# Masked keys by halves of an image, and the ends of the segments inside the edge stage of a window-attention, graph and experts kernel

## The reference, cut to what matters

```
x = x + attention(ln_c(x))      # twice over 8x8 windows: unshifted, then shifted by 4 and masked; 8 heads of 16
t = x as (32768, 128)
t = t + ffn(ln_t(t))

ffn(x): h = x @ W_gat                            # (32768, 4 heads, 4 experts)
        src, dst = edges (524288) and a loop at each node
        e = leaky_relu(a_src[src] + a_dst[dst]);  ee = exp(e - segment_max(e, dst))
        agg = segment_sum(h[src] * ee, dst) / segment_sum(ee, dst) + b_gat
        scores = layernorm(agg) averaged over heads; top 2 of 4 experts, softmax w
        out = sum over experts of w_e * (gelu(x @ W1_e + b1_e) @ W2_e + b2_e)
```

## Time and profile before

| | |
|---|---|
| median of 3 runs | 8224.57 us (8219.5 to 8226.58) |
| the profiled execution | 8225.16 us, its span 8223.3 us |
| busy, share of the span | DVE 62%, POOL 59%, PE 52%, PEld 29%, ACT 26% |
| attention, 0 to 2212 us | DVE busy 1965.09 us, PE 1807.92 us |
| edges, 2212 to 7712 us | POOL busy 4162.86 us in 4355 instructions, DVE 2771.32 us |
| 7712 to 7763 us | DVE busy 23.01 us, POOL 3.44 us |
| combine, 7763 us on | DVE busy 328.98 us, DMA engines 69% |

### The profile page before, as it was taken

One profiled execution on the slowest core, in us unless ns is written; L12 is line 12 of the kernel. 1 busy time (PEld: TensorE's weight loads), 2 busy tenths in 40 slices (PEclk: granted clock), 3 DMA queues, 4 the chain that ended last, 5 costly groups with the idle time before them and its releaser, 6 DMA issues. The chain is left out here.

```text
span 8223.3 us, 105909 instructions
## 1 busy us (share of the span) xinstructions
PE 4280.7 (52%) x31501; PEld 2348.5 (29%) x31501; DVE 5088.4 (62%) x15628; ACT 2131.3 (26%) x3826; POOL 4854.7 (59%) x5216
## 2 busy tenths in 40 slices
PE   5888888888643544535445354453544535445200
PEld 3556656556411221212212122121221212212000
DVE  9998889888745545445455454554545445455378
ACT  4666767666300100101001001010100101101034
POOL 2221112111377777777777777777777777777572
PEclk8889999999765665655656556565565655656555
DMA  1111111111211111111111111111111111111267
GB/s 48 51 51 49 50 54 52 49 55 48 62 32 37 38 32 43 32 32 43 32 43 32 32 43 32 43 32 32 43 32 43 32 32 43 32 43 32 80 202 251
DMA packets 537640, 419.78 MB, mean 51 GB/s; under 512 B 177554, under 2 KB 450498, under 8 KB 536642
## 3 DMA queue, kind: packets, MB, share of 16 engines
q1 hardware_dynamic: 323058, 323.88, 11.8%
q0 software_dynamic: 147552, 56.96, 7.0%
q10 hardware_dynamic: 66560, 33.56, 1.4%
HBM read 203.65 MB, written 176.72 MB: 46 GB/s over the span
## 5 line engine op out<-in xcount | busy, mean ns | idle before, releaser
L1326 POOL DMA_INDIRECT edge_G<-node_rows,edge_src x4352 | 4161.1, 956 | 1326.3 <-issue 1326.3
L1363 PE MATMUL edge_cbank<-edge_ohh,edge_ohl 128*128 128x256 bf16 x4096 | 1418.2, 395 | 2951.9 <-DVE edge_ohh L1496 2876.5
L1363 PEld LDWEIGHTS edge_cbank<-edge_ohh,edge_ohl 128*128 128x128 bf16 x4096 | 426.3, 104 | 3937.2 <-DVE edge_ohh L1496 3762.3
L1496 DVE TENSOR_SCALAR edge_ohh<-edge_iob,edge_dlf 128x256 bf16<-128x256 bf16 x4096 | 1196.7, 298 | 0.0
L564 POOL TENSOR_SCALAR attn_nw<-attn_mv 128x8 f32<-128x8 f32 x64 | 86.4, 1350 | 1725.5 <-DVE attn_mv L993 1725.4
L1495 DVE TENSOR_SCALAR edge_ohl<-edge_iob,edge_dlf 128x128 bf16<-128x128 bf16 x4096 | 1087.0, 266 | 14.8 <-DVE edge_dlf L1489 14.5
L1343 ACT ACTIVATE edge_hid<-edge_hbank,edge_b1c 128x512 f32<-128x512 f32 x512 | 351.6, 687 | 2498.2 <-PE edge_hbank L1370 2498.2
L1454 DVE COPY edge_O<-edge_O 128x24 f32<-128x24 f32 x64 | 12.7, 198 | 1534.6 <-DMA edge_G<-node_rows,edge_src 1534.6
L1506 DVE TENSOR_TENSOR edge_yo<-edge_ybank,edge_b2r 128x512 f32<-128x512 f32 x256 | 176.9, 691 | 946.4 <-PE edge_ybank L1379 946.4
L1346 ACT ACTIVATE edge_w<-edge_w 128x272 f32<-128x272 f32 x64 | 27.5, 429 | 2407.0 <-DVE edge_w L1468 2407.0
L1370 PE MATMUL edge_hbank<-edge_xt,edge_w 128*128 128x512 f32 x1024 | 590.2, 726 | 0.4 <-ACT edge_hid L1343 0.4
(11 more groups left out here) (239 smaller groups left out, 6383.1 us busy)
## 6 DMA issues: line engine op xcount, KB each, us to landing
edge_G<-node_rows,edge_src POOLq DMA_INDIRECT x4352, 2.4
expert_out<-edge_yo SPq DMA_DIRECT2D x64, 1024.0 KB
comb_ye<-expert_out SPq DMA_DIRECT2D x32, 2048.0 KB, 12.0
state_rows<-edge_O SPq DMA_DIRECT2D x64, 816.0 KB, 4.2
attn_km<-attn_kT SPq DMA_DIRECT2D x2048, 16.0 KB, 1.8
attn_xin<-in_x SPq DMA_DIRECT2D x32, 512.0 KB, 4.2
attn_xres<-in_x SPq DMA_DIRECT2D x32, 512.0 KB, 5.3
x_rows<-attn_x SPq DMA_DIRECT2D x32, 512.0 KB, 3.1
```

The source lines that it names most:

```text
L1326: pool.indirect_dma_start(G[b][:, t, :], None, node_rows, bass.IndirectOffsetOnAxis(ap=src[b][:, t:t + 1], axis=0)).then_inc(s_g[b][2 * t ...
L1363: pe.matmul(cbank[b][:, 0:HI], ohl[:, t % RING, :], ohh[:, t % RING, :], start=(t == 0), stop=(t == HC - 1)).then_inc(s_ohp, 1)
L1496: dve.tensor_scalar(ohh[:, t % RING, :], iob[:, :], dlf[:, 1, t:t + 1], None, ALU.is_equal).then_inc(s_oh, 1)
```

## The change

The tile of masked keys gets room for both halves of an image (8 windows each) in place of two quarters: 8 heads x 2 halves x 2 streams = 32 transfers of 32 KB in a step. Half 1 of both streams is the first thing that SP issues in a step; half 0 of the next step stands where quarter 0 stood. The block of the ends is gone: POOL makes its constants at the start of the edge block, DVE does the index of the last rows (`end_rows()`) before the scans of the last chunk and the carries (`carried()`) after them, with PE, ACT and POOL appended at the ends of their lists. The last state, first start and counts stay on chip, and so does the index, which combine reads directly. At the start of the edge block SP issues keys before weights, and DVE waits for POOL's 9 constants rather than for the weights. In diff form, cut:

```diff
@@ attention
-KRING = 2
-QWIN = 4
-QUARTERS = WGRID * WGRID // QWIN
+HWIN = WGRID * WGRID // 2
-        km = [sb(f"km{s}", [P, KRING, HEADS // 2, QWIN, WTOK]) for s in range(2)]
+        km = [sb(f"km{s}", [P, 2, HEADS // 2, HWIN, WTOK]) for s in range(2)]
-            def own_rows(s, m, q):
-                st, h, r = STREAM[s], q // 2, q % KRING
-                if q % 2 == 0:
-                    wait_free(sp, f"{s}k{h}", m)
-                if q >= KRING or m > 0:
-                    sp.wait_ge(s_sc, (m + LAG[s]) * PAIRS + 2 * (q - KRING) + 2)
-                c = (q % 2) * QWIN * WTOK
+            def own_rows(s, m, h):
+                st = STREAM[s]
+                wait_free(sp, f"{s}k{h}", m)
+                if m > 0:
+                    sp.wait_ge(s_sc, (m - 1 + LAG[s]) * PAIRS + 4 * h + 4)
                 for head in range(HEADS):
                     lo = head * HDIM
-                    sp.dma_start(km[st][lo:lo + HDIM, r, head % (HEADS // 2), :, :].rearrange("p w k -> p (w k)"),
-                                 kT[st][h][lo:lo + HDIM, c:c + QWIN * WTOK]).then_inc(s_km[st][r], 16)
+                    sp.dma_start(km[st][lo:lo + HDIM, h, head % (HEADS // 2), :, :].rearrange("p w k -> p (w k)"),
+                                 kT[st][h][lo:lo + HDIM, :]).then_inc(s_km[st][h], 16)
...
-                for s in streams(n):
-                    own_rows(s, n - LAG[s], 2)
-                for s in streams(n):
-                    own_rows(s, n - LAG[s], 3)
...
-                        for r in range(KRING):
-                            act.wait_ge(s_km[st][r], KM_DONE * (2 * m - 1 + h))
+                        act.wait_ge(s_km[st][h], KM_DONE * m)
...
-                if j % 2 == 0:
-                    pe.wait_ge(s_km[st][q % KRING], KM_DONE * (2 * m + q // 2 + 1))
+                    pe.wait_ge(s_km[st][h], KM_DONE * (m + 1))
@@ edges, SP
+            load_keys(0, 0)
+            load_keys(1, 1)
+            load_raw(0, 0)
+            load_x(0, 0)
             sp.dma_start(w1[:, :, :], W1.rearrange("e p f -> p e f")).then_inc(s_w, 16)
...
-            load_keys(0, 0)
...
+            sp.wait_ge(s_c, CONSTANTS)
+            sp.dma_start(state_rows[SORTED:SORTED + P, :], zero[:, 0:NROW]).then_inc(s_z, 16)
             chunks(sp, body)
-            sp.dma_start(last_state, O[1][:, TC, :]).then_inc(s_end, 16)
-            sp.dma_start(first_start, fmin[:, :]).then_inc(s_end, 16)
-            sp.wait_ge(s_hs, CHUNKS)
-            sp.dma_start(hist_out, hist[:, :]).then_inc(s_end, 16)
-            sp.wait_ge(s_end, 48)
+            sp.wait_ge(s_z, 16)
+            sp.wait_ge(s_new, 16)
             for b in range(2):
                 sp.wait_ge(s_st[b], 16 * CHUNKS // 2)
                 sp.wait_ge(s_yst[b], 16 * CHUNKS // 2)
@@ edges, DVE
-            dve.wait_ge(s_c, 2)
-            dve.wait_ge(s_w, 64)
+            dve.wait_ge(s_c, CONSTANTS)
...
                 outputs(b, i)
+                if last_of(b, i):
+                    end_rows()
                 st.k = 0
                 math(b, i, at + C)
+                if last_of(b, i):
+                    carried(O[b])
@@ edges, POOL
+            pool.memset(ones[:, :], 1.0).then_inc(s_c, 1)
...
             chunks(pool, body)
+            pool.wait_ge(s_end, mark["row"])
+            for b in range(2):
+                pool.wait_ge(s_st[b], 16 * CHUNKS // 2)
             pool.wait_ge(s_z, 16)
             pool.indirect_dma_start(old[:, :], None, state_rows, bass.IndirectOffsetOnAxis(ap=ri[:, 0:1], axis=0)).then_inc(s_old, 16)
-            pool.wait_ge(s_step, mark["new"])
+            pool.wait_ge(s_end, mark["new"])
             pool.indirect_dma_start(state_rows, bass.IndirectOffsetOnAxis(ap=ri[:, 0:1], axis=0), new[:, :], None).then_inc(s_new, 16)
@@ combine
-            sp.dma_start(ix[:, :], end_rows).then_inc(s_ix, 16)
-            pool.wait_ge(s_ix, 16)
```

More of the change, by code:

```diff
@@ L330, in attention @@
         s_tn = sem("s_tn")
-        s_km = [[sem(f"s_km{s}{r}") for r in range(KRING)] for s in "ab"]
+        s_km = [[sem(f"s_km{s}{r}") for r in range(2)] for s in "ab"]
         s_kz = sem("s_kz")
@@ L1201, in edges @@
         yo = [sb(f"yo{b}", [P, UTILES, EXPERTS * P]) for b in range(2)]
+        tri = sb("tri", [P, P])
+        ones = sb("ones", [P, P])
+        ident = sb("ident", [P, P])
+        rowi = sb("rowi", [P, HI], I32)
+        rowf = sb("rowf", [P, HI])
+        pref = sb("pref", [P, HI])
+        tot = sb("tot", [P, HI])
+        zero = sb("zero", [P, HI])
+        nost = sb("nost", [P, 1])
+        x3 = sb("x3", [P, 3, VCH])
+        xe = sb("xe", [VCH, 3, P])
+        most = sb("most", [VCH, P + 1])
+        total = sb("total", [VCH, P + 1])
+        w2e = sb("w2e", [VCH, 2, P])
+        car = sb("car", [P, 2, VCH])
+        old = sb("old", [P, NROW])
+        new = sb("new", [P, NROW])
+        mm = sb("mm", [P, VCH])
+        mo = sb("mo", [P, VCH])
+        wc = sb("wc", [P, 2, VCH])
+        has = sb("has", [P, 1])
+        ri = sb("ri", [P, 2], I32)
+        rf = sb("rf", [P, 4])
         hbank = [ps("hbank0"), ps("hbank1")]
@@ L1309, in _ @@
[L1309 to L1326, removed]
-                                            bass.IndirectOffsetOnAxis(ap=src[b][:, t:t + 1], axis=0)
-                                            ).then_inc(s_g[b][2 * t // TC], 16)
-            chunks(pool, body)
@@ L1679, in _, with body @@
             pool.iota(ri[:, 1:2], pattern=[[0, 1]], base=SORTED, channel_multiplier=1).then_inc(s_c, 1)
-            pool.wait_ge(s_step, mark["row"])
+            pool.wait_ge(s_dec, 1)
+            pool.indirect_dma_start(ad0[:, :], None, node_rows, bass.IndirectOffsetOnAxis(ap=first[:, :], axis=0)).then_inc(s_ad, 16)
+            def body(b, i):
+                c = 2 * i + b
+                pool.wait_ge(s_dec, c + 1)
+                if not first_of(b, i, 2):
+                    pool.wait_ge(s_math, c - 1)
+                pool.sem_inc(s_passed, 1)
+                for t in range(TC):
+                    pool.indirect_dma_start(G[b][:, t, :], None, node_rows,
+                                            bass.IndirectOffsetOnAxis(ap=src[b][:, t:t + 1], axis=0)
+                                            ).then_inc(s_g[b][2 * t // TC], 16)
@@ new lines, in _, with body @@
+        def _(act):
+            act.wait_ge(s_w, 64)
+            def body(b, i):
+                c = 2 * i + b
+                for k in range(EXPERTS * HB):
+                    act.wait_ge(s_l1, c * EXPERTS * HB + k + 1)
+                    if k == 0 and not first_of(b, i):
+                        act.wait_ge(s_l2, c * UTILES)
+                    act.activation(hid[:, k, :], hbank[k % 2][:, :], ACT.Gelu, bias=b1c[:, k:k + 1]).then_inc(s_ge, 1)
+                act.wait_ge(s_lo, c + 1)
+                act.activation(w[:, 0, :, :], w[:, 0, :, :], ACT.Exp).then_inc(s_ex, 1)
+                act.activation(wbank[:, 0:GHEADS * TC].rearrange("p (h t) -> p h t", h=GHEADS), w[:, 1, :, :], ACT.Exp).then_inc(s_ex, 1)
+            chunks(act, body)
+            act.wait_ge(s_end, mark["w2"])
+            act.activation(w2e[:, :, :], w2e[:, :, :], ACT.Exp).then_inc(s_act, 1)
+            act.wait_ge(s_end, mark["wc"])
+            act.activation(wc[:, :, :], wc[:, :, :], ACT.Exp).then_inc(s_act, 1)
```

364 lines of the change are left out of this document (143 added, 221 removed).

## The result

The kernel after takes 8043.76 us (median of 4 runs, 8042.5 to 8049.89) against 8225.58 for the kernel before beside it: a ratio of 0.9777, 95% interval 0.976 to 0.9794. That is 182 us faster. The forecast was 8092, with a range of 8066 to 8152: right in sign, too small in size, and outside the range. The profiled execution has a span of 8047.8 us, 175.5 less than before.

| stretch | before | after | less | forecast |
|---|---|---|---|---|
| attention, to the first SP issue of edges | 2212.17 | 2062.16 | 150.0 | 105 |
| from there to the first gather | 12.11 | 6.84 | 5.3 | 5 |
| first gather to the last store of state rows | 5504.07 | 5503.47 | 0.6 | 0 |
| that store to combine's first gather | 34.69 | 19.46 | 15.2 | 22.5 |
| combine, from its first gather | 460.3 | 455.9 | 4.4 | 0 |

The account below looks back on a forecast made before the run. DVE, carrying the sort, was taken to bound attention, and POOL's unbroken chain of gathers the edge stage. 8225.16 less 105 (attention), 5 (edge start) and 22.5 (ends) gave 8092.7, so 8092 for the median; range 8066 to 8152.

Parts of the forecast that it names:

- The cause of the late keys: Attention: 64 key transfers at 0.67 us take 43 us of SP's 64 us step, with quarter 2 behind two loads.
- The room before slot 4: Attention: half 1's keys were to be there at 998.1, 3.2 us before PE is ready at 1001.3.
- The rule for what comes back: Attention: per step, the smaller of PE's hold in slot 4 and DVE's idle time; 111 us with the residual, 105 taken.
- Rival (c): Attention: all DVE idle time in slots 4, 5 and at the residual goes, 152 us, for 8045; chance 0.08.
- (a): Attention: only slot 4's wait comes back, 48 us, as PE finds another wait at once, for 8150; chance 0.11.
- (b): Attention: nothing comes back, as the bytes wait for something that now comes as late, for 8198; chance 0.04.
- (d): Attention: transfer pace follows bytes, 1.34 us per 32 KB, so keys come later and the kernel slows to 8520; chance 0.04.
- Clearing and half 0: Attention: doubled clearing delays first scores 3.6 us but stays hidden; half 0 keeps its pace and causes no wait.
- Start of the edge stage: Edge stage's start: keys before weights, and waiting for POOL's constants, make it 5 us earlier, bounds 3 and 6.
- The ends: Last scans to combine's first gather: folding the ends block away saves 22.5 us of 34.7, bounds 15 and 24.
- Next block 0.4: End of the edge block: after the scatter's landing, the next block starts 0.4 us later.
- The sum: Whole kernel: 8225.16 - 105 - 5 - 22.5 = 8092.7, or 8092 for the median of the runs.

Follow-up runs that it names:

- e9_order: The kernel before with two lines moved, issuing quarter 2 of the masked keys ahead of the two loads; 8083.28 us, ratio 0.9817.
- e7_behind: The kernel after with half 1 of the masked keys issued behind the two 512 KB loads, where quarter 2 stood; 8210.49 us, ratio 0.9973.
- e11_warm3: The kernel before with 112 extra PE matmuls in slot 4, ahead of the wait for stream B's masked keys; 8193.65 us, ratio 0.9946.
- e10_busy4: The kernel after with 164 extra PE matmuls in slot 4 of steps 4 to 30; 8133.24 us, ratio 0.9874.
- e4_drain: The kernel after with one explicit POOL drain right behind the last gather of the edge stage; 8039.21 us, ratio 0.9776.

## Why the prediction was wrong in size and right in sign

**The cause of the late keys: wrong.** "Why are the keys late?" was answered with the number of transfers, 43 us of SP's 64 in a step, with "two loads of 512 KB" mentioned as if only their issue stood in the way. SP's idle 8.4 us ahead of the load were missed, since only the transfers' own rows were read and not the waits of the queue. `e9_order` has all 64 transfers and the whole gain; `e7_behind` has 32 and none of it. The forecast of the early keys still came out, since the change moves half 1 ahead of the loads as well: a right result by a partly wrong reason, and so in part luck. The room before slot 4 was to be 3.2 us; in the step shown it is 944.19 - 942.6 = 1.6.

**The rule for what comes back: the failed step.** The smaller of two numbers, how long PE was held and how long DVE stood idle, gave 111 us, of which the forecast took 105. Attention gave 150.0 (154 by the two other profiles): 133.2 in slots 4 and 5 and at the residual (152.6 us of DVE's idle time became 19.4), 7.3 from shorter DVE busy time, 9.5 from DVE's other waits. The rule takes PE to work after the wait as fast as without it. It didn't: the grant was 0.50, and with the waits gone PE needs 59 us less for the same matmuls. So the sum lacked a term for the low clock, and that term measured between 44 us (`e11_warm3`) and 73 to 77 (`e10_busy4`). The wait itself, at a high clock, cost 106 us in the first of them, near the 111 of the rule, and 73 to 77 in the second, under it. The profile offered a sign: the earlier trace rows has the grant at 0.91, and the grant around a wait was not looked up. Rival (c), "all idle time at these places goes", had the total, 8045, with a chance of 0.08, but not the reason: 133 of its 152 us went, the rest came from other places, and the low clock isn't in it. That its number fits is in part luck.

**Rivals (a), (b) and (d): refuted.** DVE's waits of slots 5 and at the residual went with that of slot 4. The pace didn't follow the bytes: 589 ns at 16 KB and at 32 KB, landing 1.8 and 2.0 us. The Trainium skill says in DMA: Bandwidth & Descriptors, section Issuing engines are not separate DMA queues, that the time to initiate a DMA is usually small relative to the DMA itself. For this form the traces don't agree: 0.59 us to issue beside 1.8 to 2.0 to land, and SP's pace, a median of 0.63 us from one start to the next, is set by the issue. Yet what the prediction drew from it, that half as many and larger transfers win nothing, is what `e7_behind` measured, for another reason: the place in the queue.

**Clearing and half 0: right in effect.** The two clearings took 3.5 us each. The first scores came at 41.2 us, 9 later than before and not 3.6, and DVE took its first at 59.0 (58.9 before): hidden. Half 0 never was waited for once the steps ran full.

**Start of the edge stage: right**, 5.3 us for 5, with the constants and not the keys as the last thing waited for.

**The ends: right up to the scatter, wrong behind it.** The scatter was to come 9.35 us after the store and came 8.94 after it, with landings of 2.5 and 2.2 for 2.4. "Next block 0.4" failed: POOL's drain ended 7.4 us after the scatter's landing. In the kernel before it was hidden under the last scans, and in the 31.80 us of POOL's idle time it can't be seen. With the drain moved, `e4_drain` has 12.20 us from store to gather, 22.5 less than before, the number of the forecast.

**The sum.** The forecast was 45 us too little in attention, 7.3 too much at the ends, and 5.0 in the gathers' chain and combine, where nothing was forecast and the kernels' own spread is as large.

## What to carry to other kernels

When a transfer is late, look first at what its queue stands still for, and at the wait of whatever stands ahead of it: moving two lines past a load that waits was worth as much as the larger tile and the halved count. Price a stall of PE with the granted clock around it, in windows of a few microseconds, since the slow work after the wait was a third to a half of the price here. When blocks are folded together, ask what their ends did under cover: the drain of POOL after more than four thousand indirect DMAs took 8.4 to 8.6 us here, and it could be done where another engine was still busy.

## What the runs showed of the hardware that was not expected

- PE's granted clock fell from 1.00 to 0.50 in a wait of 4.4 us and was back at 1.00 in the stretch from 1011, with work from 1005.68 on. 1.1 us of matmuls ahead of the same wait, in each step, made attention 27 us shorter; 3 us of them 44.
- Matmuls of 64 rows by 64 columns that go round the four quarters of the array start four at a time, 0.109 us from group to group: 164 of them, bf16 with 256 columns, held PE for 4.47 us, 0.027 us each. The duration recorded for one is 0.27 us, so it doesn't tell what many cost.
- The drain of POOL after its last instruction took 0.07 us with no indirect DMA since the last drain, 1.3 with 2, 5.3 to 5.7 with 256, 8.4 to 8.6 with 4353 or more. In the kernel after POOL had been idle for 21 us ahead of its last two, and that didn't shorten it.
